# Cross attention of the next batch as tile jobs inside the expert part of a Trainium2 kernel

## What is computed

```
scores = einsum('bqd,bkd->bqk', layernorm(x), ctx) / sqrt(512)      # 512 x 77 for each batch
scores = where(mask, -1e9, scores); att = softmax(scores)
x2 = x + einsum('bdl,ol->bdo', swapaxes(att @ ctx, -1, -2), W_merge) + b_merge
h  = layernorm(x2)
rw = gating(h, sim_matrix, gates)                   # 16 weights for each row
q, k, v = [einsum('bte,bted->btd', rw, einsum('btc,ecd->bted', h, p)) for p in (q_proj, k_proj, v_proj)]
attn = softmax(causal(q k^T / 8)) v                 # within a batch
out = x2 + einsum('bted,edc->btc', attn[:, :, None, :] * rw[..., None], o_proj)
```

## Time and profile before

| what | value |
|---|---|
| three runs, median (lowest to highest) | 992.86 us (987.39 to 992.89) |
| the profiled execution, its own time | 990.36 us |
| its span, first to last instruction | 988.6 us, mean granted clock 0.959 |
| PE busy / DVE / ACT / POOL | 924.0 / 619.8 / 232.6 / 173.7 us |
| moved by DMA | 53.68 MB, 54 GB/s over the span |

### The profile page before, as it was taken

The page is one execution under the profiler, slowest core; times in us unless marked ns, Lnnn a source line. Parts: engine busy times, 40 slices in busy tenths (PEclk is TensorE's granted clock), DMA queues, the critical chain, the costliest instruction groups (busy, mean ns, idle before and its releaser), DMA issues.

```text
span 988.6 us, 15673 instructions
## 1 busy us (share of the span) xinstructions
PE 924.0 (93%) x5000; PEld 844.8 (85%) x5000; DVE 619.8 (63%) x1747; ACT 232.6 (24%) x543; POOL 173.7 (18%) x344
## 2 busy tenths in 40 slices
PE   4787866999999999999999999999999999999987
PEld 3455544999999999998999999999999999999976
DVE  7788773666565656565656575747574657565743
ACT  6666651121111111111111121111111111111111
POOL 4554443530101110101010010101010101001100
PEclk9788886999999999999999999999999999999997
DMA  5454623110202020101010101010101010100010
GB/s 177 150 184 161 213 87 117 65 54 2 64 1 65 1 64 1 65 1 55 10 55 9 54 11 53 11 54 11 53 11 54 11 48 16 48 17 29 26 40 24
DMA packets 30574, 53.68 MB, mean 54 GB/s; under 512 B 7241, under 2 KB 7241, under 8 KB 30386
## 3 DMA queue, kind: packets, MB, share of 16 engines
q1 hardware_dynamic: 30514, 53.01, 15.7%
HBM read 36.22 MB, written 16.78 MB: 54 GB/s over the span
## 4 chain that ended last, share of the span: by engine, by line
PE 77%; DVE 4%; issue 2%; DVEq 0%; ACT 0%; POOL 0%; POOLq 0%
PE psQ L1254 51%; PE psO L1341 17%; PE psM L1327 2%; PE psT L1293 2%; PE psT L1229 1%; PE psT L1265 1%; PE psT L1274 1%; PE psQ L1341 1%; DVE acc L1114 1%; PE psM L1311 1%; DVE resid L1144 0%; PE psM L1308 0%; PE psT L1282 0%; DVE neg_mx L1148 0%; DVE b_stats L1059 0%
## 5 line engine op out<-in xcount | busy, mean ns | idle before, releaser
L1254 PE MATMUL psQ<-Wqkv_hi,hT_hi 128*128 128x384 f32 (+1 forms) x1024 | 352.9, 345 | 1.4 <-DVE hT_lo L1055 1.4
L1254 PE MATMUL psQ<-Wqkv_lo,hT_hi 128*128 128x384 f32 (+1 forms) x1024 | 347.3, 339 | 0.0
L1254 PE MATMUL psQ<-Wqkv_hi,hT_lo 128*128 128x384 f32 (+1 forms) x1024 | 347.1, 339 | 0.0
L1114 DVE SCALAR_TENSOR_TENSOR acc<-psQ,RW,acc 128x192 f32<-128x192 f32 x448 | 165.6, 412 | 235.2 <-PE psQ L1254 234.0
L1254 PEld LDWEIGHTS psQ<-Wqkv_hi,hT_hi 128*128 128x128 f32 x1024 | 193.3, 189 | 3.6 <-DVE hT_lo L1055 1.8
L1254 PEld LDWEIGHTS psQ<-Wqkv_lo,hT_hi 128*128 128x128 f32 x1024 | 193.2, 189 | 2.1
L1254 PEld LDWEIGHTS psQ<-Wqkv_hi,hT_lo 128*128 128x128 f32 x1024 | 192.8, 188 | 0.0
L891 POOL TENSOR_TENSOR pow_tmp<-b_mv,eps 128x1 f32<-128x1 f32 x32 | 6.1, 190 | 560.9 <-DVE b_mv L1061 560.8
L1341 PE MATMUL psO<-Wo_hi,mixedT_hi 128*128 128x512 f32 x248 | 98.8, 398 | 0.0
L1341 PE MATMUL psO<-Wo_lo,mixedT_hi 128*128 128x512 f32 x248 | 97.5, 393 | 0.0
L1341 PE MATMUL psO<-Wo_hi,mixedT_lo 128*128 128x512 f32 x248 | 97.4, 393 | 0.0
(11 more groups left out here) (167 smaller groups left out, 1253.7 us busy)
## 6 DMA issues: line engine op xcount, KB each, us to landing
X<-in_x SPq DMA_DIRECT2D x8, 1024.0 KB, 5.4
x_scratch<-XR SPq DMA_DIRECT2D x16, 512.0 KB, 2.9
X<-x_scratch SPq DMA_DIRECT2D x32, 256.0 KB, 2.7
resid<-x_scratch SPq DMA_DIRECT2D x32, 256.0 KB, 3.2
out<-resid SPq DMA_DIRECT2D x32, 256.0 KB, 2.1
stage<-in_w_qkv SPq DMA_DIRECT2D x8, 768.0 KB, 6.3
mixed_f<-in_w_o SPq DMA_DIRECT2D x8, 256.0 KB, 3.2
CTX<-in_ctx_in SPq DMA_DIRECT2D x8, 154.0 KB
```

Of the source, the lines that this page charges most:

```text
L1114: dve.scalar_tensor_tensor(out=acc[e][:], in0=src, scalar=w, in1=acc[e][:], op0=ALU.mult, op1=ALU.add).then_inc(expert_added, 1)
L1254: last = pe.matmul(psQ[g % 4][:, 0:first_col(g) + PW], x[:, c * P:(c + 1) * P], w[:, c, E + g * PW - first_col(g):E + (g + 1) * PW], start ...
```

## The change

The two blocks become one. Only batch 0's cross attention (and the first tile of batch 1) stands ahead of the slots, as straight code. All else of the cross attention is cut into jobs of one tile and hung into the slots of the expert part: in tile t, slot 0 loads nothing but transposes the raw rows of tile t+5 (`X1_T_SLOT`), slot 2 makes its scores (`x1_score`: now the rows are the stationary operand and the 78 columns of the context are streamed, so the scores come out untransposed, 12 matmuls a tile instead of 12 of 512 columns a batch), slots 3 and 4 finish the softmax weights, slot 1 makes x2 of tile t+1 (`sum_x2`), which no longer comes back from HBM. G of the next batch is summed in slots 15, 17, 19, 21, one tile each, with W_merge parts reloaded from HBM (`merge_scratch`). The next context is centred and transposed in slots 19 and 20. All new PE results but G go through the same two `psT` banks. The expert and output weights are loaded whole by ACT's queue; ACT and DVE split them, `Wqkv` in the first eight slots, `Wo` in slots 9 to 23.

The projection now goes by chunk pairs: each mixed pair is at once multiplied for both tiles of the half, the even one into `psO`, the odd one into `psM`, the bank of scores and values. `mixedT` holds four chunks instead of eight and `mixed_f` is one buffer. The attention's slots move by one or so.

```diff
-QK_T_AT = {12: 0, 16: 1, 28: 2, 0: 3}
-SCORES_AT = {16: 0, 18: 1, 29: 2, 2: 3}
...
+QK_T_AT = {12: 0, 16: 1, 28: 2, 1: 3}
+SCORES_AT = {16: 0, 18: 1, 30: 2, 3: 3}
...
-          7: (1, 0), 8: (1, 1), 9: (1, 2), 10: (1, 3)}
+          8: (1, 0), 9: (1, 1), 10: (1, 2), 11: (1, 3)}
-PROJECT_AT = {27: [(0, 0)], 28: [(0, 1)], 30: [(1, 0), (1, 1)],
-              11: [(2, 0)], 12: [(2, 1)], 14: [(3, 0), (3, 1)]}
+PROJECT_AT = {k + 2: job for k, job in MIX_AT.items()}
+SUM_SLOT, NORM_SLOT, H_T_SLOT = 1, 3, 5
+X1_T_SLOT, X1_SCORE_SLOT, X1_INV_SLOT, X1_LOW_SLOT = 0, 2, 3, 4
+G_AT = {15: 0, 17: 1, 19: 2, 21: 3}
+X1_LEAD = 5
...
+                def load_x1(t1, q):
+                    sp.wait_ge(qkv_summed, PAIRS * (t1 - X1_LEAD) - 1)
+                    sp.dma_start(H[:], row(x, t1)).then_inc(x1_in, 16)
+                    sp.dma_start(MASK[:, q, :], row(mask, t1)).then_inc(x1_in, 16)
+                def load_merge(n, q):
+                    sp.wait_ge(G_part, TILES + n)
+                    for part in range(2):
+                        sp.dma_start(merge[part][:].bitcast(F32), merge_dram[q, part]).then_inc(merge_in, 16)
...
+                    if n == 2:
+                        pool.wait_ge(sim_floored, 1)
+                        pool.tensor_tensor(sim_rn, sim_ss, half_e, ALU.pow).then_inc(sim_rooted, 1)
...
+                for g in range(PAIRS):
+                    act.dma_start(W_raw[:, :, w_cols(g)], w_qkv[:, :, g * PW:(g + 1) * PW]
+                                  ).then_inc(ld_w[g], 16)
...
+                def x1_moments(t1, p, tile):
+                    dve.bn_stats(x1_stats[:], tile)
+                    dve.drain()
+                    dve.bn_aggr(x1_mv[:], x1_stats[:])
...
+                def add_x2(t):
+                    n = moves.step()
+                    dve.wait_ge(moved, n)
...
+                    dve.tensor_tensor(X2[:], psT[moves.bank()][:], X2[:], ALU.add).then_inc(moved_lo, 1)
+                    dve.wait_ge(moved_lo, n)
+                    dve.bn_stats(stats[:], X2[:])
...
+                def x1_score(p, rows_moved):
+                    bank = next_bank(moved_lo, rows_moved, has_high=False)
+                    for c in range(KC):
+                        for n, (a, w) in enumerate(products(hT[p], ctxT)):
+                            last = pe.matmul(bank[:, 0:CP], a[:, c * P:(c + 1) * P], w[:, c, :],
...
+                def sum_x2(t, b):
+                    pe.wait_ge(G_lo, b + 1)
+                    bank = next_bank(cs_lo, t + 1, has_high=False)
+                    for n, (a, w) in enumerate(products(cs, G)):
...
+                        if attn and k in PROJECT_AT:
...
+                            pe.wait_ge(mix_lo, 4 * h2 + u + 1)
+                            for i in range(2):
+                                for c in range(2):
+                                    for n, (a, w) in enumerate(products(mixedT, Wo)):
```

More of the change, by code:

```diff
@@ L128, in cross_attention_then_experts_kernel @@
+        simn = [w[:, :, 0:E] for w in Wv]
+        G = (sb("G_hi", [CP, D], F32R), G_lo_over)
+        cs = (sb("cs_hi", [CP, P], F32R), cs_lo_over)
         ident = sb("ident", [P, P])
@@ L1351 @@
-OWN_STEPS = 4 * (3 + 5) + 4
+        eps = sb("eps", [P, 1])
+        ctxT = pair("ctxT", [P, KC, CP])
+        MASK = sb("MASK", [P, TILES, C], U8)
+        limit = [sb(f"limit{p}", [P, C]) for p in range(2)]
+        sc = [sb(f"sc{p}", [P, C]) for p in range(2)]
+        room = sb("room", [P, C])
+        att = pair("att", [P, TILES, CP])
+        merge = pair("merge", [P, D])
+        x1_stats = sb("x1_stats", [P, 6])
+        x1_mv = sb("x1_mv", [P, 2])
+        x1_var = [sb(f"x1_var{p}", [P, 1]) for p in range(2)]
@@ new lines, in cross_attention_then_experts_kernel @@
+        kT_lo = sb("kT_lo", [P, S], F32R)
+        probs = [sb(f"probs{p}", [P, S]) for p in range(2)]
+        probsT_all = pair("probsT", [P, 7 * P])
+        probsT = [[part[:, 0:(4 * h + 3) * P] for part in probsT_all] for h in range(2)]
+        attT = [sb(f"attT{h}", [P, 2 * P]) for h in range(2)]
+        gates_q = sb("gates_q", [P, (TILES + 1) * 64])
+        gatesT = sb("gatesT", [P, S], F32R)
+        spread = sb("spread", [P, OC, P], F32R)
+        mixed_f = sb("mixed_f", [P, 2, 2 * P])
@@ new lines, in cross_attention_then_experts_kernel @@
+        sim_ss, sim_rn, gate_e, half_e = [attT[0][:, 2 * KC * E + n * E:2 * KC * E + (n + 1) * E] for n in range(4)]
+        ones_f, causal_f = attT[1][:, 0:P], attT[1][:, P:2 * P]
+        psQ = [ps(f"psQ{k}") for k in range(4)]
+        psT = [ps(f"psT{k}") for k in range(2)]
+        psM = ps("psM")
+        psO = ps("psO")
+        ld_ctx = [sem(f"ld_ctx{n}") for n in range(2)]
+        ld_x = [sem(f"ld_x{n}") for n in range(X1_LEAD)]
+        ld_mask = sem("ld_mask")
+        ld_merge = [sem(f"ld_merge{n}") for n in range(TILES)]
@@ new lines, in is_first, with live, job_lists, first_col @@
+        def is_first(b):
+            return isinstance(b, int) and b == 0
+        def live(n, limit_n):
+            return not isinstance(n, int) or n < limit_n
+        def job_lists(k, b, qkv, lead):
+            j, g = divmod(k, PAIRS)
+            prepare = qkv and live(TILES * b + j + 1, N_TILES)
+            cross = qkv and live(TILES * b + j + X1_LEAD, N_TILES)
+            own = k >= LEAD
+            return j, g, prepare, cross, (qkv if own else lead), (b if own else b - 1)
+        def first_col(g):
+            return E if g == 0 else 0
@@ new lines, in tile_copies, with place, keys_of, v_twice @@
+        def tile_copies(k, qkv, lead):
+            if k in QK_T_AT and (lead if k < 2 else qkv):
+                return QK_T_AT[k]
+            return None
+        def place(i):
+            return slice((1 - i % 2) * P, (2 - i % 2) * P)
+        def keys_of(half, i):
+            blocks = 2 * (i - i % 2) + 3
+            return half.rearrange("p (s l) -> p s l", l=P)[:, 1 - i % 2:blocks:2, :]
+        def v_twice(i):
+            return nat[i % 2][:, 4 * DH:5 * DH].unsqueeze(1).broadcast_to([P, 2, DH])
```

2029 lines of the change are left out of this document (950 added, 1079 removed).

## The result

The changed kernel takes 1039.05 us (median of four runs, 1037.83 to 1040.0) against 992.0 for the kernel before (the median of four runs by now, 987.39 to 992.89); the ratio is 1.0488, 95% interval 1.046 to 1.0517. I had forecast 988, with 966 to 1010 as the range. The profiled execution took 1037.83 us, of which the span is 1036.1; that of before had a span of 988.6, so there are 47.5 us to explain, and 50.7 against my sum of 985.4 for the span.

A forecast was written before the change was run, and what follows sets the result against it. PE was taken as the bound from 169 to 958 us, with latency chains before and after. 46 + 7 + 819.4 + 90 + 24 - 1 = 985.4 for the span, 987.2 with 1.8 around it; forecast 988 us, range 966 to 1010.

The forecast's parts named there:

- the sum itself: Whole span: all terms added to 985.4 us, with projection, mixes and expert matmuls unchanged in number.
- Term 1: New head before the first expert matmul: that matmul starts at 46 us, bounds 40 to 58, replacing 169.2 us.
- The remark on bias rows beside weights in flight: Head: by the skill's shared DMA engines, bias rows land late beside 8 MB of weights; sum 3.4 us larger.
- Term 2: Tile 0: PE runs short of weight pieces split by ACT and DVE; +7 us, 2 to 12.
- Term 3: Full part: PE work moved in, with scores 0.11 us apart, costs 90 us; 74 with 0.06.
- Term 4: Slots 10, 2, 18 and 26: new PE waits for a psT bank, 18 + 5 + 1 = 24 us, 8 to 36.
- that cover: Outside the tight places of slots 2, 10, 18 and 26, other work was said to hide PE's waits.
- Term 5: The end: projection by pairs starts near 971.9 instead of 973.1, same 48 matmuls; -1 us, -2 to +2.
- The mask: Rival, 15%: the raw tile's mask lands late, delaying DVE's moments and PE's transposes in slot 0; 40 us, giving 1028.
- The fourth: Rival, 10%: head and tile 0 at upper bounds (58 and 12), or DVE a microsecond later in tight places; 1005.
- the second: Rival, 30%: bank waits mostly absent, 972, or score matmuls 0.06 apart, 972; with both 956.

The follow-up runs named there:

- the best version: The version of 7 without moving the raw tile's moments, weight pieces four slots ahead of use, two of them ahead of the context; 968.28 us.
- experiment 4: The changed kernel with PE's waits filled by issuing expert and score matmuls again, in slots 1, 10, 20 and 26; 1034.49 us.
- experiment 1: The changed kernel with the ten weight loads issued by SP behind the second context load, in place of ACT; 1029.87 us.
- experiment 2: The changed kernel with DVE's adds of slots 0 and 1 moved to slot 2, behind the read-out of x2; 1012.48 us.
- 6: The changed kernel with weight loads from SP, adds of slots 0 and 1 in slot 2, and the loop over batches written out; 984.46 us.
- 7: The version of 6 with x2's moments and the raw tile's moments later on DVE, and the context's transposes in slot 22; 982.47 us.
- experiment 9: The same run as the best version: the version of 7 less the raw tile's moments move, with earlier weight pieces; 968.28 us.
- 3: The changed kernel with the loop over batches written out on all engines; 1024.1 us.
- 5: The changed kernel with only the high by high product of the cross scores, 4 of 12 matmuls a tile; 1020.3 us.

## Why the prediction was wrong

**The failed step is the sum itself**: "Projection, mixes and expert matmuls keep their number", and with it, tacitly, their price. They cost 31.4 us more (table). In the best version, which has the same instructions and hardly a wait, 8.1 of these are left: expert slots, projections and mixes in shorter runs, with the psO and psM halves of a pair by turns. The other 23 went with the waits. By the one-microsecond windows PE lost 22 us of full speed from 62 us to 1005 us, against none in the same part of the kernel before (behind the hand-over, where the 400-column matmuls of both start 0.33 us apart for some 4 us), so most of it is the clock. I wrote down waits at their length and never asked what PE does behind them; experiment 4 shows for seven of the eight stretches that it is the pause that does it.

**Term 1 (46, bounds 40 to 58)**: 55.7. The ten issues took 14.5 us, not 5, and moving them gave 6.5 (experiment 1). I had taken 0.3 to 1.0 us for an issue; one of 768 KB takes 1.6. Of the 3 us left, 1.3 are the scores of the raw tile at half pace (0.21 apart). The low part of a weight piece, which I put at 1.7 (three times 0.69 is 2.07), takes 1.76 (median of eight). The remark on bias rows beside weights in flight was not put to the test by the changed kernel, where the weights had landed before; in experiment 1 such rows took 3.5 and 5.4 us.

**Term 2 (+7)**: PE waits 6.2 us for weight pieces in tile 0. Right.

**Term 3 (90)**: 94.3. The scores are 0.11 apart, as taken from the earlier trace rows, and not 0.08; a set costs 1.28 in the best version, 1.40 in the changed kernel. Right.

**Term 4 (24, bounds 8 to 36)**: 31.5 from 100 to 910 us (10.2 + 7.9 + 7.4 + 5.3 + 0.4 + 0.3) and 2.1 in the last body, in the range, but in part by other places. Slot 10 has 15.1 for 18 with that of the last body, slot 2 some 2 for 5. Unforeseen were 7.4 in slot 1 at the turns, where the kernel before has only a wait for ACT, and 5.3 within the context's transposes, whose second bank waits for the probabilities moved in the same slot. I had called that cover held.

**Term 5 (-1)**: nothing. From the last expert matmul to the end are 30.8 us, 30.9 before. The projection does start 1.0 us earlier (14.5 behind that matmul for 15.4), after a wait of 0.68 for the first low part, but its 48 matmuls take 0.8 longer: two mixes stand among them, and seven of their starts are at the pace of half clock where there were six:

```profile
1019.75 0.77 PE L1288 MATMUL psO<-Wo_hi,mixedT_hi 128*128 128x512 f32 x1 [0.68 <-DVE mixedT_lo L1055]
```

The sum of the misses: 9.7 for the head, 4.3 for new work, 5.5 for idle time (35.5 for the 30 of terms 2, 4 and 5), 31.4 for old work, 50.9 for 50.7.

**The rivals.** The mask does not come late: its loads land in 2.3 us (shortest, median, longest),

```profile
DMA to landing us min/median/max: 2.1/2.3/6.4
```

and no engine waits for one in the bodies. The fourth, with 1005, had the right sign at about a third of the size, and of its places the head (55.7 for its 58) but not tile 0 (6.2 for 12). Of the second, the half on cheap scores is refuted by their spacing of 0.11. The half without bank waits, at 972, was not the changed kernel; the best version has hardly such a wait and takes 968, but with other lists and without the loop, which by itself gave the kernel before 6 to 8 us, so this does not bear the rival out.

## What to carry to other kernels

Price a wait of the bound engine at its length and at what comes behind it: here 31.5 us of waits cost about 19 more in clock (18.8 in the eight stretches). Before work is moved into a full engine's list, walk the list of the engine that hands back its buffers, and put first what the full engine waits for; one table entry was worth 26.6 us, more than half of the loss. And look for waits that only loop turns have, since each stands once in the code and several times in the run.

## What the runs showed of the hardware

- The granted clock fell behind pauses of PE that were far from long: behind 1.1 to 1.4 and 0.9 us with 1.5 us of thin matmuls between them in all six bodies, behind the 2.5 us of the loop's turns in two of three. Behind a lone pause of 0.9 it fell in some bodies and not in others (experiment 2: after 437.15, not after 681.66), and behind the 0.4 to 1.0 us that are left in the bodies of experiments 6, 7 and 9 it never did. Once, in experiment 4, it fell with no pause at all before it.
- In the changed kernel's profile the head has a granted clock of 1.00, though its 400-column matmuls start 0.33 us apart at 57 us and 0.18 later. Experiments 1 and 9 show the same. The other versions have 0.50 there, from about 46 us on in experiments 2, 3 and 4 and from 37, 36 and 30 us in 5, 6 and 7, with the same 0.33 between these matmuls. The spacing of rows is the surer reading.
- DVE stood 2.7 us at each turn of the loop (1.8 in the kernel before), with no wait shown.
- Ten loads issued by ACT in a row held it for 14.5 us; the 768 KB ones take 1.6 us each (median of eight, 0.6 to 2.4), and the same from SP (0.6 to 3.1). The Trainium skill ("DMA: Bandwidth & Descriptors", Rules for kernel authors) says that spreading DMAs over engines saves only issue time; that time is what counted here.
